# The last mixture of experts with W2 stationary in two float32r parts

## The reference

```
logits = x @ router_W + router_b
w, idx = top_k(logits, 2);  w = softmax(w)
gates  = one_hot(idx, 8) combined with w          # (tokens, 8)
xhat   = (x - mu) * rsqrt(var + EPS)
h      = xhat[:, :, None, :] * ln_g + ln_b        # one affine per expert
a      = gelu(h @ W1 + b1, approximate=False)     # (tokens, 8, 512)
y      = a @ W2 + b2 + x[:, :, None, :]           # (tokens, 8, 128)
out    = sum over experts of y * gates
```

## Time and profile before

| | us |
|---|---|
| median of 3 runs | 2481.97 |
| lowest and highest | 2480.72, 2484.28 |
| profiled execution, its own time | 2475.36 |
| its span | 2473.6 |
| PE busy | 2078.5 (84%) |
| DVE busy | 1605.4 (65%) |
| ACT busy | 999.2 (40%) |
| POOL busy | 655.3 (26%) |
| first up matmul of the last stage to the end | 2026.3 to 2473.6 |

### The profile page before, as it was taken

How to read it: one execution, slowest core, us unless ns; L and a number is a source line. 1 busy time by engine, 2 the same in 40 slices (tenths; PEclk the granted TensorE clock), 3 DMA queues, 4 the chain that set the end, 5 groups by cost and what they waited for, 6 DMA issues and landing times. The chain is left out here.

```text
span 2473.6 us, 46736 instructions
## 1 busy us (share of the span) xinstructions
PE 2078.5 (84%) x16920; PEld 1650.4 (67%) x16920; DVE 1605.4 (65%) x4182; ACT 999.2 (40%) x1990; POOL 655.3 (26%) x409
## 2 busy tenths in 40 slices
PE   4888888884799988999768885889689869999998
PEld 3667767664456655666556774678477758888887
DVE  5776676774777737777377678677767775333344
ACT  2455455453155552555432222233223334444443
POOL 3545545543145551555400003000300010000000
PEclk9999999997599996999889998899899969999999
DMA  4111111111000000000000001000000020000000
GB/s 154 70 69 58 61 63 65 65 69 36 0 1 2 1 1 1 1 2 1 1 1 0 0 0 41 1 1 1 1 1 1 1 79 5 4 4 4 4 4 8
DMA packets 34795, 54.88 MB, mean 22 GB/s; under 512 B 7104, under 2 KB 16960, under 8 KB 33856
## 3 DMA queue, kind: packets, MB, share of 16 engines
q1 hardware_dynamic: 34624, 52.57, 5.8%
HBM read 16.90 MB, written 2.10 MB: 8 GB/s over the span
## 5 line engine op out<-in xcount | busy, mean ns | idle before, releaser
L1051 POOL TENSOR_TENSOR mb_psum<-mb_pt 128x1024 f32<-128x1024 f32 x112 | 267.1, 2387 | 313.5 <-ACT mb_pt L1031 312.8
L1031 ACT ACTIVATE mb_pt<-mb_stb 128x1024 f32<-128x1024 f32 x256 | 249.2, 1021 | 146.7 <-PE mb_stb L1132 146.2
L2332 PEld LDWEIGHTS md_bk<-md_w,md_a 128*128 128x128 f32 x2048 | 264.0, 192 | 26.2 <-ACT md_a L2179 3.9
L2179 ACT ACTIVATE md_a<-md_bk,md_b 128x512 f32<-128x512 f32 x256 | 175.5, 687 | 244.9 <-PE md_bk L66 244.5
L919 DVE TENSOR_REDUCE mb_mxp<-mb_p1b 128x1 f32<-128x512 f32 x352 | 231.1, 683 | 65.9 <-PE mb_p1b L1116 62.0
L2332 PE MATMUL md_bk<-md_w,md_a 128*128 128x128 f32 x2048 | 267.9, 276 | 2.7 <-DVE md_acc L2276 2.1
L2276 DVE SCALAR_TENSOR_TENSOR md_acc<-md_bk,md_gate,md_acc 128x128 f32<-128x128 f32 x256 | 71.9, 344 | 235.9 <-PE md_bk L2332 235.8
L351 DVE TENSOR_TENSOR ma_tr<-ma_pbank,ma_cs 128x512 f32<-128x512 f32 x256 | 161.6, 682 | 73.3 <-PE ma_pbank L66 69.2
L1955 ACT ACTIVATE mc_p<-mc_sb,mc_nb 128x512 f32<-128x512 f32 (+3 forms) x160 | 98.0, 621 | 186.9 <-DVE mc_nb L1843 186.9
L495 ACT ACTIVATE ma_e<-ma_sbank,ma_mx 128x80 f32<-128x80 f32 x512 | 120.3, 385 | 117.5 <-DVE ma_mx L358 117.5
L2033 PE MATMUL mc_pv<-mc_v,mc_pt 128*128 128x128 f32 x1088 | 149.8, 282 | 11.7 <-DVE mc_pt L1892 11.4
(11 more groups left out here) (329 smaller groups left out, 4838.3 us busy)
## 6 DMA issues: line engine op xcount, KB each, us to landing
ma_swp<-ma_tr SPq DMA_DIRECT2D x256, 128.0 KB, 2.0
mg_X<-x SPq DMA_DIRECT2D x4, 512.0 KB, 10.4
ma_cs<-cs SPq DMA_DIRECT2D x1, 2048.0 KB, 9.4
mc_cs<-cs SPq DMA_DIRECT2D x1, 2048.0 KB, 8.1
md_raw<-d_w SPq DMA_DIRECT2D x1, 2048.0 KB, 7.3
md_w<-d_w SPq DMA_DIRECT2D x1, 2048.0 KB, 10.9
out<-mg_X SPq DMA_DIRECT2D x8, 256.0 KB, 2.3
ma_raw<-w_qkv SPq DMA_DIRECT2D x1, 1536.0 KB, 8.4
```

What stands on the lines that cost most here:

```text
L1031: nc.scalar.activation(pt[:, T % RING, :, :].rearrange("p (b h) q -> p b (h q)", b=2), stb[:, 2 * (i % 2):2 * (i % 2) + 2, :], ACT.Exp, sc ...
L1051: nc.gpsimd.tensor_tensor(psum[:, n % SUMS, :, :], pt[:, T % RING, :, :], pt[:, (T + 1) % RING, :, :], ALU.add).then_inc(summed, 1)
L2179: nc.scalar.activation(a[:, e % 2, c, :], ub[:, c, :], ACT.Gelu, bias=b1[:, e, c:c + 1]).then_inc(gelu, 1)
L2332: last = nc.tensor.matmul(db[:, e % 2, s * P:(s + 1) * P], a[:, e % 2, c, s * P:(s + 1) * P], w2[:, e, c, :], start=(c == 0), stop=(c == F ...
```

## The change

All of it is in `ffn_layer1`.

- W2 is also split into `w2h` (ACT, eight copies) and `w2l` (POOL, eight subtractions). It arrives in a tile `late`, which is reused afterwards.
- ACT still applies Gelu, now into one buffer of four quarters. The output is split too: ACT copies quarters 0 to 2 into `ah`, DVE quarter 3, and DVE subtracts to get `al`.
- `down(j, c)` holds `w2h` and `w2l` stationary and moves `ah` and `al`, 512 tokens at a time, in three passes; the result is feature-major, `db[j % 2]` [128 features, 512 tokens].
- In that layout a gate is a value per column. PE turns the gates of a block into `gT` (8 rows of 512), and for each expert and block SP issues one DMA that spreads row `e` over 128 partitions into one of four buffers `gb`, each with its own semaphore. DVE computes `(db + b2) * gb` in one instruction (`scale`), into `accT` for the first expert and into `tmp` for the others, and POOL adds `tmp` to `accT`.
- PE turns each block's `accT` back (`turn_back`), and DVE finishes the block row tile by row tile, in parts that are spread over the items of later blocks.
- The loops over blocks are gone: every stream is written out over 64 items `j` (block `j // 8`, expert `j % 8`), and PE goes from one block into the next without a wait for the last.

```diff
+GB = 4
+GATE_AT = 3
+STORE_AT = (2, 6)
+POWER_AT = (1, 4)
+APPLY = (10, 12)
+FINISH_AT = 2 * (NE + 2)
...
+                for j in range(ITEMS):
+                    n, e = divmod(j, NE)
+                    if e == 0:
+                        sp.wait_ge(gT_done, n + 1)
+                    if j >= GB:
+                        sp.wait_ge(scaled, j - GB + 1)
+                    sp.dma_start(gb[:, j % GB, :], gT[e:e + 1, n % 2, None, :].to_broadcast([1, P, BLK])).then_inc(gb_in[j % GB], 16)
+                    if e == STORE_AT[1] and n >= STORE_AT[0]:
+                        store(n - STORE_AT[0])
...
+                act.wait_ge(w2_in, 16)
+                for e in range(NE):
+                    nc.scalar.activation(w2h[:, e, :, :], w2raw[:, e, :, :], ACT.Copy).then_inc(w2_hi, 1)
...
+                turn_gates(0)
+                for j in range(ITEMS):
+                    n, e = divmod(j, NE)
+                    hidden(j, 0)
+                    hidden(j, 1)
+                    high(j, 0)
+                    hidden(j, 2)
+                    high(j, 1)
+                    hidden(j, 3)
+                    high(j, 2)
+                    if e == GATE_AT and n + 1 < NBLK:
+                        turn_gates(n + 1)
...
+                for e in range(NE):
+                    pool.wait_ge(w2_hi, e + 1)
+                    nc.gpsimd.tensor_tensor(w2l[:, e, :, :], w2raw[:, e, :, :], w2h[:, e, :, :].bitcast(F32),
+                                            ALU.subtract).then_inc(w2_lo, 1)
+                for j in range(ITEMS):
+                    n, e = divmod(j, NE)
+                    if e > 0:
+                        pool.wait_ge(scaled, j + 1)
+                        if e > 1:
+                            pool.wait_ge(added, n * (NE - 1) + e - 1)
+                        nc.gpsimd.tensor_tensor(accT[:, n % 2, :], accT[:, n % 2, :], tmp[:, e % 2, :],
+                                                ALU.add).then_inc(added, 1)
...
+                def scale(j):
+                    n, e = divmod(j, NE)
+                    dve.wait_ge(down_mm, (j + 1) * FC)
+                    dve.wait_ge(gb_in[j % GB], 16 * (j // GB + 1))
...
+                    nc.vector.scalar_tensor_tensor(dst, db[:, j % 2, :], b2[:, e:e + 1], gb[:, j % GB, :], ALU.add,
+                                                   ALU.mult).then_inc(scaled, 1)
...
+                for j in range(ITEMS):
+                    low(j, 0)
+                    low(j, 1)
+                    finish_at(2 * j)
+                    high(j, 3)
+                    low(j, 2)
+                    if j > 0:
+                        scale(j - 1)
+                    low(j, 3)
+                    finish_at(2 * j + 1)
...
+                def down(j, c):
+                    n, e = divmod(j, NE)
+                    if c == 0:
+                        if n == 0:
+                            pe.wait_ge(w2_lo, e + 1)
+                        if j >= 2:
+                            pe.wait_ge(scaled, j - 1)
...
+                    pe.wait_ge(lo_done, j * FC + c + 1)
+                    matmul_split(nc, db[:, j % 2, :], w2h[:, e, c, :], w2l[:, e, c, :], ah[:, c, :], al[:, c, :],
+                                 start=(c == 0), stop=(c == FC - 1)).then_inc(down_mm, 1)
...
+                for c in range(FC):
+                    up(0, c)
+                turn_gates(0)
+                for j in range(ITEMS):
+                    n, e = divmod(j, NE)
                     for c in range(FC):
-                        up(0, c)
-                    for e in range(NE):
-                        for s in range(BPT):
-                            if e + 1 < NE:
-                                up(e + 1, s)
-                            down(e, s)
-                    pe.wait_ge(gelu, (n + 1) * NE * FC)
-                    pe.wait_ge(acc_done, n * NA + NA)
+                        if j + 1 < ITEMS:
+                            up(j + 1, c)
+                        if c == 2 and e == GATE_AT and n + 1 < NBLK:
+                            turn_gates(n + 1)
+                        if c == 2 and e == 1 and n > 0:
+                            turn_back(n - 1)
+                        down(j, c)
+                turn_back(NBLK - 1)
```

More of the change, by code:

```diff
@@ L2135, in ffn_layer1 @@
         ln = m.sem("ln")
+        w2_in = m.sem("w2_in")
+        w2_hi = m.sem("w2_hi")
+        w2_lo = m.sem("w2_lo")
         up_mm = m.sem("up_mm")
         gelu = m.sem("gelu")
+        hi_act = m.sem("hi_act")
+        hi_dve = m.sem("hi_dve")
+        lo_done = m.sem("lo_done")
         down_mm = m.sem("down_mm")
-        acc_done = m.sem("acc_done")
+        scaled = m.sem("scaled")
+        added = m.sem("added")
+        gT_mm = m.sem("gT_mm")
+        gT_done = m.sem("gT_done")
+        gb_in = [m.sem(f"gb_in{k}") for k in range(GB)]
+        turned = m.sem("turned")
+        row_sum = m.sem("row_sum")
         stored = m.sem("stored")
-        NA = BPT * (1 + 2 * NE)
+        ITEMS = NBLK * NE
+        HIA = FC - 1
         group = range(GRP)
@@ L2184, in _ @@
                 stats_pool(nc, pool, S)
-                with pool.Fori(0, NBLK) as n:
+                for e in range(NE):
[10 more added lines that the diff above has]
+                                                ALU.add).then_inc(added, 1)
+                    if e == POWER_AT[1] and n >= POWER_AT[0]:
+                        F.pool(nc, pool, n - POWER_AT[0], S)
+                for n in range(NBLK - POWER_AT[0], NBLK):
                     F.pool(nc, pool, n, S)
@@ new lines, in finish @@
+                def finish(n, part):
+                    s = part // 2
+                    if part < 2 * BPT:
+                        if part % 2 == 0:
+                            residual(n, s)
+                            total(n, s)
+                        else:
+                            dve.wait_ge(row_sum, n * BPT + s + 1)
+                            F.row_stats(nc, dve, n, s, acc)
+                    elif part in APPLY:
+                        for k in range(2):
+                            s = 2 * APPLY.index(part) + k
+                            F.apply(nc, dve, n, s, acc, X, n * BPT + s)
@@ L2282, in _ @@
+                scale(ITEMS - 1)
+                for t in range(2 * ITEMS, FINISH_AT + 2 * NE * (NBLK - 1) + PARTS):
+                    finish_at(t)
             @block.tensor
@@ new lines, in _, with turn_gates, up @@
+                pe.wait_ge(c_in, 16 * 2)
+                def turn_gates(n):
+                    pe.wait_ge(summed, 1)
+                    if n > 0:
+                        pe.wait_ge(gT_done, n)
+                    for s in range(BPT):
+                        last = nc.tensor.transpose(gtb[:, s * P:(s + 1) * P], gate[:, n * BPT + s, :], ident[:, :])
+                    last.then_inc(gT_mm, 1)
+                def up(j, c):
+                    n, e = divmod(j, NE)
+                    cols = slice(n * BLK, (n + 1) * BLK)
+                    cs = slice(c * P, (c + 1) * P)
+                    if j >= 1:
+                        pe.wait_ge(gelu, (j - 1) * FC + c + 1)
+                    matmul_split(nc, ub[:, c, :], wh[:, e, cs], wl[:, e, cs], nh[:, cols], nl[:, cols]).then_inc(up_mm, 1)
```

150 lines of the change are left out of this document (87 added, 63 removed).

## The result

The changed kernel takes 2636.5 us (median of 4 runs, 2632.8 to 2638.9) against 2483.1 us (2480.7 to 2484.8) for the kernel before on the same chip: a ratio of 1.062, 95% interval 1.060 to 1.064, slower by 153 us. Its profiled execution took 2635.4 us, with a span of 2633.6. The forecast was 2703 us, slower, in a range of 2425 to 2740. Only the wider range, made to hold the rivals too, has it.

The account below looks back on a forecast made before the run. PE was taken to bound the last stage; in the changed kernel broadcasts would: first issue 2042, 64 x 9.85 plus latency and stores to 2678, tail 17, span 2695, 221 more; 2482 + 221 = 2703 us, range 2425 to 2740.

Parts of the forecast that it names:

- The deciding term: Last stage, gate broadcasts: each reads 262,144 bytes out of one partition, takes 9.85 us and cannot hide under 5.7 us.
- The rate: Gate broadcast: one partition's side passes what one DMA engine passes, 26.6 GB/s of 426 for all 16.
- The step that failed: Expert items of the last stage: four buffers hide latency but not rate, so every item's period becomes 9.85 us.
- The first issue: Start of the expert items: first broadcast issued at 2042 us, with the router 4 us later through POOL's W2 split.
- The tail: End of the stage: scaling, add, transposes, row tiles and the remaining output steps, 17 us behind the last landing.
- TensorE's item: One expert on one block on PE: 24 matmul starts 0.233 us apart, 5.60 us, plus 0.12 for transposes.
- The first rival: Last stage: broadcast hidden, under 5.7 us, and PE bounds; span 2424, time 2432 us, faster by 2%; chance 0.20.
- The second rival: Last stage: broadcast hidden, DVE and POOL block each other, 6.2 us an item; 2467 us, faster by 0.6%; chance 0.14.
- The lock: DVE's two-operand SBUF subtraction stands still until POOL's add is done: 1.83 us instead of 0.68.
- The third rival: Last stage: PE at 1.2 GHz throughout, 656 us in place of 362; 2726 us; chance 0.02.
- The signs named ahead: Last stage: landings over 20 us, even period near 9.9, PE busy 60%, DMA 27 GB/s, L2367's idle ended by DMA.
- The rule cited with a row: Gate broadcast: the skill's 27.6 GB/s for partitions 0 to 3 gives 9.50 us each and a sum 22 us less.

Follow-up runs that it names:

- x_once: Changed kernel with only the first four of its 64 gate broadcasts made, later scalings reusing those buffers; 2451.9 us.
- x_spread: Changed kernel with each broadcast replaced by a transfer of the same 256 KB read from all 128 partitions, gates left out; 2440.1 us.
- x_ports4: Changed kernel with gate rows copied onto all 128 partitions, broadcasts taking turns over four copies 8 partitions apart; 2441.6 us.
- x_row0: Changed kernel with all 64 broadcasts reading gate row 0, in partition 0; 2697.5 us.
- x_rows03: Changed kernel with broadcasts reading gate rows 0 and 3 in turn, whatever the expert; 2701.9 us (one run).
- x_same32: Changed kernel with gate rows copied onto all 128 partitions, broadcasts alternating between two copies 32 partitions apart; 2638.3 us.
- x_ports4_early: x_ports4 with the split of W2 (ScalarE's copies, GpSimd's subtractions) moved ahead, behind the first four copies of normalized rows; 2435.1 us.
- x_wide1: x_ports4_early with more of the first two items done under the router, and each broadcast reading all sixteen copies of its row; 2423.5 us.

## Why the prediction was right, and where it was not

**The deciding term, right in kind.** The forecast put the period of an item on the broadcast out of one partition, and x_once, x_spread and x_ports4 each take that away in another way and fall to 5.7 us an item (x_once once its four broadcasts are through; its mean over all is 5.85). The rate, bounded only from a row of all 16 engines together, was 26.6 GB/s; x_row0 measures 9.84 us an item with the stores in it.

**The step that failed** is "the period of every item becomes 9.85". It holds while the source stays among the same four partitions. The gates of experts 0 to 3 lie in partitions 0 to 3, those of 4 to 7 in partitions 4 to 7, and at each change between them two broadcasts overlap, twice a block. Broadcasts and their latency were put at 636 us from the first issue (2042 to 2678); x_row0 took 631.9 (2045.01 to 2676.9), the changed kernel 569.6 (2048.18 to 2617.80). That is 66 us of the error by itself. The prediction gave 0.04 to a broadcast between 5.7 and 9 us, and the mean of 8.85 is there.

The trace has a semaphore event for each sixteenth of a broadcast. In x_row0 the first sixteenth of a broadcast lands 8.2 to 8.4 us behind the last of the one ahead (the first twelve), and so it does in the changed kernel for its first four, numbers 0 to 3. But there the first of broadcast 4 lands 0.3 us behind the last of broadcast 3, and those of 8 and 12 land 6.6 and 4.8 us ahead of the last of 7 and 11.

The rate rested on an analogy, that a partition's side passes "what one engine passes", and that it came within 1% is luck as far as these runs go. The busy share of 0.87 is a mean over all 16 engines, so all of them took part, and what they shared was the way out of a group of partitions (x_rows03, x_same32), not one partition's side. Why this way has the rate of one engine, no run here shows.

**The other terms of the sum.** The first issue came at 2048.2 instead of 2042: 4.4 us because the stage began later, for reasons outside the change, 1.3 more because the router came 5.3 us later after the load instead of the 4 taken (x_ports4_early gives 5.2 of them back by moving the split of W2), and 0.5 between the router and the issue. The tail was 15.8 us from the last scaling (2617.80) to the end, against 17. In sum +6.2 - 66.4 - 1.2 = -61.4, and 2695 - 61.4 = 2633.6, the span. The other 5 us of the 67 are not of the kernel: I added 6.6 us for the distance of the median from the profiled run, and here it was 1.1. That x_row0's span of 2692.7 is so near the sum's 2695 is in part luck: its first issue came 3.0 us late, its broadcasts took 4.1 less and its tail 1.2 less.

**TensorE's item** was put at 5.60 + 0.12; the hidden kernels show 5.71 with starts 0.232 us apart through up and down alike.

**The first rival** (broadcast hidden, 2432 us) is what x_spread and x_ports4 are: 2440.1 and 2441.6. Its condition, a broadcast of less than 5.7 us an item, was the right one. The trace of x_ports4 ends 10.3 us behind the 2424 of that sum. Its first down matmul starts at 2050.94 instead of 2045 (2.6 of this is the stage's later start, 1.1 the router), from there to the end of the last one it takes 367.8 us instead of 362, part of it at the low clock, and its tail is 1.4 us shorter. The estimate of 2.6 us for a landing that stands with this rival fits x_spread's 2.3, and not a broadcast out of one partition, which took 10.1 at the least in x_ports4. **The second rival** (VectorE and GpSimd, 6.2 us an item) is ruled out: in x_spread VectorE is busy 81.7% and TensorE 99.1%. The lock itself is as in the earlier trace rows. Here it stretches both sides, GpSimd's add to 1.66 us on average and L2347 to 0.83, as at one spot of the changed kernel:

```profile
2318.35 2.96 DVE L2347 TENSOR_TENSOR md_al<-md_raw,md_ah 128x512 fp32r<-128x512 f32 x3
2318.51 1.65 POOL L2264 TENSOR_TENSOR md_late<-md_late 128x512 f32<-128x512 f32 x1 [6.49 <-DVE md_late L2367]
```

**The third rival** (TensorE at 1.2 GHz throughout) did not come about either. After a wait the clock is low and then full again (TensorE's timeline of the changed kernel; matmuls start 0.43 us apart at first and 0.23 later):

```profile
2309.43 0.77 PE L64 MATMUL md_bk<-md_ah,md_w2h 128*128 128x512 f32 x1 [3.79 <-DVE md_al L2347]
...
2310.43 0.63 PE L66 MATMUL md_bk<-md_al,md_w2h 128*128 128x512 f32 x1
2310.85 0.63 PE L64 MATMUL md_bk<-md_nh,md_wh 128*128 128x512 f32 x1
...
2313.00 0.39 PE L64 MATMUL md_bk<-md_nh,md_wh 128*128 128x512 f32 x1
2313.23 0.40 PE L65 MATMUL md_bk<-md_nh,md_wl 128*128 128x512 f32 x1
```

The granted clock was 0.88 in the two windows of the changed kernel shown above, and in x_row0, with longer waits, 0.83 to 0.85; its period stayed at the broadcast's 9.84.

**The signs named ahead.** Landings over 20 us: 29.7. DMA near 27 GB/s: 34, since 256 KB per 8.85 us are 29.6 and a store of 256 KB per 70.8 us adds 3.7. An even period near 9.9: not even in the changed kernel, and in x_row0 and x_rows03 even but for the pair at each store. TensorE busy at 60%: 77 to 79%, because the period was shorter and because at the low clock each record is longer. Idle time before L2367 "ended by the DMA": only 20 us of 242 are put under that name.

**The rule cited with a row.** The Trainium skill's figure for partitions 0 to 3 (SBUF — State Buffer, "Door 1: The DMA port swizzle") would have given 9.50 us; 9.72 to 9.79 was measured between scalings. But another part of that section of the Trainium skill, that neighbours in fours share a port and the next four have another, was the more useful one: it fits the two overlaps a block. I took the number and did not walk the eight source rows along the table there, which would have shown where the 66 us are.

## What to carry to other kernels

A DMA that replicates one SBUF row over 128 partitions reads it 128 times out of one place: price it by the bytes at its source, 256 KB at 26.8 GB/s, and not by what lands. More buffers should not help, since the queue was always full (not run); several copies of the row in different groups of partitions (8 apart, not 32), or one pass through DRAM, do. And where many sources are to be had, put them into each transfer instead of taking turns: the rate is enough either way, but only then is the first one early.

## What the runs showed of the hardware that was not expected

- The shared limit follows the partition number in a way that distance alone doesn't tell: 0 and 3 share (9.84 us an item), e and e + 32 share (2638.3 us), e and e + 8 don't (2443.0 us).
- The busy share of the DMA engines doesn't tell their rate: 0.87 at 34 GB/s, 0.82 at 52 and 0.14 at 52 GB/s, in three kernels that move the same bytes.
- An issue waits for the transfers ahead of it. On SyncE's queue a store's issue took 9.74 us in the changed kernel and 0.59 in x_wide1; what else stands in that queue pays for slow transfers:

```profile
2233.54 9.74 SPq L2184 DMA_DIRECT2D out<-mg_X  x1
```

```profile
2204.35 0.59 SPq L2186 DMA_DIRECT2D out<-mg_X  x1
```
